# Attention row maxima transposed whole and split into two parts out of PSUM, and an inner maximum joined over two columns

## The reference

```python
x = x + _L0_xattn_ref(_layernorm(x), ctx, ...)   # cross attention without values
x = x + _L0_ffn_ref(_layernorm(x), w_gate, w_up, w_down)
x = x + _L1_xattn_ref(_layernorm(x), ctx, ctx)
x = x + _L1_ffn_ref(_layernorm(x), gate_w, w0, w1, wo, ...)   # 8 experts, 2 per token

# inside _L0_ffn_ref, before each of its matmuls:
def act_quant(x):
    scale = 127.0 / jnp.clip(jnp.max(jnp.abs(x), axis=-1, keepdims=True), EPS)
    return jnp.clip(jnp.round(x * scale), -128.0, 127.0) / scale

# _L1_xattn_ref: 32 query heads of 16 dims, 8 key/value heads, 4 query heads on each
scores = jnp.einsum('bkgsd,bktd->bkgst', qh, kh) / scale
weights = jax.nn.softmax(scores, axis=-1)
out = jnp.einsum('bkgst,bktd->bkgsd', weights, vh)
```

## Time and profile before

| | us |
|---|---|
| median of three runs | 1726.64 |
| lowest and highest | 1716.98, 1729.44 |
| the profiled execution | 1717.66 |
| its span, first to last instruction | 1715.8 |
| busy PE, DVE, ACT, POOL | 1581.2, 957.0, 715.6, 700.8 |
| attention (first to last maximum and its end) | about 495 to 952 |
| mixture of experts, to the end | about 952 to 1716 |

### The profile page before, as it was taken

One profiled execution on the slowest core, in us unless ns is written; L12 is line 12 of the kernel. 1 busy time (PEld: TensorE's weight loads), 2 busy tenths in 40 slices (PEclk: granted clock), 3 DMA queues, 4 the chain that ended last, 5 costly groups with the idle time before them and its releaser, 6 DMA issues. The chain is left out here.

```text
span 1715.8 us, 24430 instructions
## 1 busy us (share of the span) xinstructions
PE 1581.2 (92%) x8105; PEld 1051.9 (61%) x8106; DVE 957.0 (56%) x1571; ACT 715.6 (42%) x1157; POOL 700.8 (41%) x478
## 2 busy tenths in 40 slices
PE   6869999999779999999988399999999999999998
PEld 4555656575533433433333378788878888878886
DVE  6998889797878897888874512222222222222221
ACT  6884646464537777777765111111111111111111
POOL 1124342543503125362464482680754080740065
PEclk9879999999988999999998799999999999999999
DMA  9189600000321445253520343241441041431078
GB/s 356 76 305 386 236 1 1 1 0 1 108 65 46 121 126 148 81 150 89 146 97 33 143 136 114 83 172 37 172 156 53 25 178 31 172 126 34 25 131 213
DMA packets 90945, 196.17 MB, mean 114 GB/s; under 512 B 7153, under 2 KB 9074, under 8 KB 90226
## 3 DMA queue, kind: packets, MB, share of 16 engines
q1 hardware_dynamic: 71746, 156.68, 27.3%
q0 software_dynamic: 7168, 17.04, 4.4%
q10 hardware_dynamic: 11952, 21.43, 3.8%
HBM read 113.28 MB, written 81.32 MB: 113 GB/s over the span
## 5 line engine op out<-in xcount | busy, mean ns | idle before, releaser
L2002 DVE TENSOR_REDUCE neg_max<-psum 128x2 f32<-128x1024 f32 x256 | 300.7, 1219 | 54.6 <-PE psum L2642 53.6
L1388 ACT ACTIVATE probabilities<-psum 128x512 f32<-128x512 f32 x512 | 270.8, 601 | 105.4 <-PE psum L2669 101.1
L2120 DVE TENSOR_TENSOR expert_inner<-psum,expert_inner 128x512 f32<-128x512 f32 x78 | 53.9, 691 | 393.9 <-ACT expert_inner L1481 393.9
L2812 PE MATMUL psum<-expert_weight_parts,sorted_tokens_t_first 128*128 x624 | 252.4, 405 | 9.9 <-POOL expert_weight_parts L1020 6.5
L2813 PE MATMUL psum<-expert_weight_parts,sorted_tokens_t_first 128*128 x624 | 248.5, 398 | 0.0
L2814 PE MATMUL psum<-expert_weight_parts,sorted_tokens_t_second 128*128 x624 | 248.5, 398 | 0.0
L1481 ACT ACTIVATE expert_inner<-psum 128x512 f32<-128x512 f32 x78 | 46.7, 599 | 401.8 <-PE psum L2814 401.8
L2669 PE MATMUL psum<-query_rows,key_rows 50*128 50x512 f32 x512 | 180.7, 449 | 8.1 <-ACT probabilities L1388 5.6
L2642 PE MATMUL psum<-key_rows,query_rows 48*128 48x512 f32 x512 | 174.3, 499 | 13.8 <-DVE neg_max L2002 11.2
L2812 PEld LDWEIGHTS psum<-expert_weight_parts,sorted_tokens_t_first 128*128 128x128 f32 x624 | 119.0, 191 | 38.8 <-issue 11.9
L2680 PE MATMUL psum<-probabilities,value_and_one 128*32 128x512 f32 x1024 | 142.2, 629 | 0.0
(11 more groups left out here) (304 smaller groups left out, 2952.3 us busy)
## 6 DMA issues: line engine op xcount, KB each, us to landing
sorted_x<-zero_rows SPq DMA_DIRECT2D x9, 3960.0 KB, 30.4
w_of_odd_expert<-in_L_ffn_w SPq DMA_DIRECT2D x8, 2048.0 KB, 9.1
wo_of_expert<-in_L_ffn_wo SPq DMA_DIRECT2D x7, 2048.0 KB, 8.7
query_rows<-query_rows_of_units SPq DMA_DIRECT2D x64, 192.0 KB, 3.6
w_of_even_expert<-in_L_ffn_w SPq DMA_DIRECT2D x6, 2048.0 KB, 12.1
sorted_tokens<-sorted_x ACTq DMA_DIRECT2D x39, 264.0 KB, 2.8
sorted_y<-expert_out ACTq DMA_DIRECT2D x39, 256.0 KB, 2.1
query_rows_of_units<-dims_first SPq DMA_DIRECT2D x32, 256.0 KB
```

The source lines that it names most:

```text
L1388: nc.scalar.activation(prob[t % 2][:, i * SEQ:(i + 1) * SEQ], bank[4 + n % 3], ACT.Exp, scale=HD ** -0.5).then_inc(c_e, 1)
L2002: nc.vector.tensor_reduce(of_pair[:, p, st, :], ring(("max", (m, i))).rearrange("p (h n) -> p h n", h=2), AX.X, ALU.max, negate=True).then ...
L2120: nc.vector.tensor_tensor(h, bank[2 * half + 1], h, ALU.mult).then_inc(e_h, 1)
L2812: nc.tensor.matmul(out_bank, hi[:, cols], w_r[:, bass.ds(w_at, 512)], start=start, stop=False)
```

## The change

The maxima are transposed as they are, 16 columns of `nm`, as soon as the eight reductions are done (PE waits for `c_red` in place of `c_np`). `neg_max_split` and `nm_parts` with its memset go. The split is made by DVE out of PSUM: a copy to `first` (signals `c_nhi`), a wait for it, and a subtraction of `first` from the PSUM tile to `second` (signals `c_nsb`). SP issues one DMA for the first part's rows of both halves behind `c_nhi`, and one for the second part's behind `c_nsb`. In `inner_scales` the two columns are joined by one `tensor_reduce` over the two columns.

```diff
             def neg_max_rows(m):
-                sp.wait_ge(c_nsb, m + 1)
-                for h in range(2):
-                    row = 64 * h + 3 * HD
-                    sp.dma_start(q_r[m % 4][row:row + 2, :].bitcast(F32).rearrange("p (t n) -> p t n", n=P),
-                                 nm_t[m % 2][16 * h:16 * h + 16, :].bitcast(F32)).then_inc(c_nmd[m % 4], 16)
+                for part, (made, of) in enumerate(((c_nhi, nm_t[m % 2][0]), (c_nsb, nm_t[m % 2][1]))):
+                    sp.wait_ge(made, m + 1)
+                    rows = q_r[m % 4][3 * HD + part::64, :].bitcast(F32)
+                    sp.dma_start(rows.rearrange("h (t n) -> h t n", n=P),
+                                 of[:].bitcast(F32)).then_inc(c_nmd[m % 4], 16)
...
-                c.step(nc.vector.tensor_tensor(am2[:, s], am2_half[:, 0:1], am2_half[:, 1:2], ALU.max))
+                c.step(nc.vector.tensor_reduce(am2[:, s], am2_half[:], AX.X, ALU.max))
...
-                if there(m):
-                    neg_max_split(m)
...
-                dve.wait_ge(c_red, 8 * (m + 1))
-                dve.wait_ge(c_nt, m)
-                c.step(nc.vector.tensor_copy(parts[:, :, 0, :], of_head))
-                nc.vector.tensor_tensor(parts[:, :, 1, :], of_head, parts[:, :, 0, :], ALU.subtract).then_inc(c_np, 1)
...
             def neg_max_out(m):
+                of = ring(("negmax", m))[0:2 * ST * 2, 0:P]
+                first, second = nm_t[m % 2]
                 dve.wait_ge(c_nt, m + 1)
                 if m >= 2:
                     dve.wait_ge(*neg_max_loaded(m - 2))
-                nc.vector.tensor_copy(nm_t[m % 2][:], ring(("negmax", m))[0:32, 0:P]).then_inc(c_nsb, 1)
+                nc.vector.tensor_copy(first[:], of).then_inc(c_nhi, 1)
+                dve.wait_ge(c_nhi, m + 1)
+                nc.vector.tensor_tensor(second[:], of, first[:], ALU.subtract).then_inc(c_nsb, 1)
...
             def neg_max_transposed(m):
                 job = ("negmax", m)
-                pe.wait_ge(c_np, m + 1)
+                pe.wait_ge(c_red, 8 * (m + 1))
                 take(job, c_nsb, m + 1)
-                nc.tensor.transpose(ring(job)[:, 0:P], nm_parts[:].bitcast(F32), ident[:]).then_inc(c_nt, 1)
+                nc.tensor.transpose(ring(job)[0:2 * ST * 2, 0:P], nm[m % 2][:], ident[:]).then_inc(c_nt, 1)
```

More of the change, by code:

```diff
@@ L243, in network @@
         nm = [small.tile(f"neg_max{i}", [P, ST * GROUP]) for i in range(2)]
-        nm_parts = small.tile("neg_max_parts", [P, P], F32R)
-        nm_t = [small.tile(f"neg_max_rows{i}", [32, P], F32R) for i in range(2)]
+        nm_t = [[small.tile(f"neg_max_{part}_rows{i}", [2 * ST * 2, P], F32R) for part in ("first", "second")] for i in range(2)]
         att_r = small.tile("attended_rsum", [P, ST * GROUP])
@@ L364, in network @@
         c_rows, c_nmd = [sem(f"c_rows{i}") for i in range(4)], [sem(f"c_nmd{i}") for i in range(4)]
-        c_mx, c_red, c_np, c_nt, c_nsb = sem("c_mx"), sem("c_red"), sem("c_np"), sem("c_nt"), sem("c_nsb")
+        c_mx, c_red, c_nhi, c_nt, c_nsb = sem("c_mx"), sem("c_red"), sem("c_nhi"), sem("c_nt"), sem("c_nsb")
         c_s, c_e, c_pv, c_oe, c_at, c_eo, c_v = (sem("c_s"), sem("c_e"), sem("c_pv"), sem("c_oe"), sem("c_at"),
@@ L708, in routing_constants @@
             def routing_constants():
-                sp.wait_ge(c_ones, 6)
+                sp.wait_ge(c_ones, 5)
                 sp.dma_start(gw[:].rearrange("p (k e) -> p k e", k=DC)[:, :, 0:EXPERTS],
@@ L2216, in phase_c @@
                 dve.wait_ge(c_xt, CTX_CHUNK + 1)
-                nc.vector.memset(nm_parts[:].bitcast(F32), 0.0).then_inc(c_ones, 1)
                 nc.vector.memset(gw[:], 0.0).then_inc(c_ones, 1)
@@ L2222, in phase_c @@
                 queries_deviation(BATCH - 1)
-                dve.wait_ge(c_ones, 6)
+                dve.wait_ge(c_ones, 5)
                 for u in range(UNITS + 1):
```

3 lines of the change are left out of this document (removed).

## The result

| | us |
|---|---|
| before, median of six runs beside the changed kernel | 1724.05 (1716.98 to 1729.44) |
| after, median of six runs | 1707.05 (1697.96 to 1708.86) |
| ratio | 0.9889, 95% interval 0.9862 to 0.9916 |
| the profiled execution after | 1707.91, span 1706.1 |

The changed kernel is 1.1% faster, 17.0 us at the medians, where the prediction had 8.0. The measured time, 1707.05, lies inside the stated range of 1706 to 1728, near its fast end; the gain is twice the one forecast, and three terms of the sum had the wrong size, which the part on the prediction takes up one by one.

A forecast was written before the change was run, and what follows sets the result against it. PE was taken as the bound in steady attention (busy 98.10 of 100 us), with time won there reaching the end whole. Terms -1 - 1 - 5.0 - 0.8 - 0.2 = -8.0 us from 1726.64 gave 1718.6, range 1706 to 1728.

The forecast's parts named there:

- the inner maximum: L1891 in phase_b, stalled beside POOL: its replacement by a reduction wins -0.2 us, bound -2.25.
- the regular units: Steady attention, 29 units: split leaves the place ahead of the reductions; -1 us in all, bounds -7.5 and +7.5.
- the stalls of the split: L2031's subtraction held up beside POOL: -5.0 us for the one at 879.15 and -0.8 for the rest.
- the small stalls: L2031's remaining stalls, 1.7 us together on DVE, half counted as reaching PE: -0.8 us.
- A slip of up to 0.26 us against the weight load: Tile 3 in a regular unit: c_nsb comes 0.33 us later, so tile 3 can start at R + 0.74.
- The rival of this name: Late c_nsb decides: tile 3 waits 0.26 us a unit, giving 1727.1, or 1730.6 with a dearer subtraction; chance 0.12.
- The long stall: L2031's 4.50 us subtraction at 879.15 behind POOL's L1020 goes, and its unit with it shortens: -5.0 us.
- The rival that the stall lands elsewhere: L1020 meets L2074 longer, 3 to 4 us, so the 5.0 shrinks to 1 to 2: 1722 to 1723; chance 0.18.
- by that row the stall moves on to L1892: phase_b: the one-column TENSOR_SCALAR behind the inner maximum stalls like four-column L1991, leaving some 0.1 us a tile.
- The start: First two units, where DVE sets the pace: 3 splits of 0.30 us and a memset less; -1 us, bounds 0 and -1.2.
- The anchor: Forecast counted from 1726.64, the median of the runs shown, 9 us above the profiled execution.
- clock case: Fewer waits spare slow-clock stretches, 3 to 10 us more, plus the inner-maximum and regular-unit bounds: 1700 to 1712; chance 0.22.

The follow-up runs named there:

- After with small scatters: The changed kernel with the eight indirect DMAs of each of batches 0 and 1 replaced by plain 16 x 16 DMAs; 0.9877 of before.
- before with small scatters: The kernel before with the eight indirect DMAs of each of batches 0 and 1 replaced by plain 16 x 16 DMAs; 0.9997 of before.
- two reductions there: The changed kernel with two small reductions of the 16 columns where the old split stood; 0.9960 of before.
- wide transpose: The changed kernel with neg_max in tiles of 128 columns, 112 of them zero, all transposed (also called 128 columns); 0.9882 of before.
- one more copy: The changed kernel with one more copy of 16 x 128 out of PSUM ahead of the second part; 0.9857 of before.
- three copies: The changed kernel with three more copies of 16 x 128 out of PSUM ahead of the second part; 1.0018 of before.
- split put back: The changed kernel with the old split's copy and SBUF subtraction back in their place, written where nobody reads; 0.9979 of before.
- the table's first four rows: Profiles of before, before run again (0.9982), before with plain small DMAs for scatters (0.9997), and before with only the inner maximum changed (0.9969).
- after again: The changed kernel, unchanged, run and profiled a second time; 0.9887 of before.
- attention only: The kernel before with the new handling of the maxima but the old inner maximum; 0.9921 of before.
- scatters later: The changed kernel with POOL's two scatters of batch 0 in units 17 and 18 in place of 15 and 16; 0.9871 of before.

## Why the prediction was right or wrong

**The sum, by its terms.** The prediction had which changes win, and three sizes wrong: the inner maximum (-0.2, measured -5.3), the regular units (-1, measured -7.0) and, the other way, the stalls of the split (-5.8, some -3.7). Undoing and separating gives 5.3 us for the inner maximum and 13.5 for the attention, at the medians. What the 13.5 are made of has to come from single profiles. After with small scatters against before with small scatters is the pair that no scatter disturbs: 4.8 us up to the first reciprocal, 10.4 in units 1 to 26, 4.6 in 27 to 29, nothing behind, 19.8 in all. 3.4 of the 10.4 is one unit of that execution of before (unit 21, 16.82 for 13.40) at a mean clock of 0.70, which leaves 7.0. And 1.8 of these are unit 9 alone, 15.26 for 13.49, whose mean clock was 0.89 in every profile of the old attention and 1.00 in most of the new; a small stall of L2031, 0.46 us at 639.89 in before, stands in that unit, but with two reductions there, which don't stall, it took 15.71, so that its part in the clock isn't shown. Of what the prediction asked to see, L2031's successor near 0.30 us and never long came, the unit around 880 took 15.95 us (some 17 predicted), and "wrong if regular units change by more than 0.2 us" came true.

- *Regular units, -1, and the small stalls, -0.8.* Mis-sized, and the largest miss: 7.0 us over units 1 to 26 in that pair. The bound stood in the prediction (7.5) and I took next to nothing of it. Two steps failed. The 0.26 us that I called "the most a regular unit can win" is the idle time of PE's matmul; the weight load ahead of it had idled 0.58 at the same instant and idles 0.21 now, and a chunk unit won 0.41. And I let PE's busy 98.10 in 100 stand for a bound, where the wide transpose shows that 0.1 us more work of PE a unit costs nothing. Plain units did win little, 0.08. Putting 0.34 us of reductions back took all but 0.02 us of both away, so the place is the cause.
- *"A slip of up to 0.26 us against the weight load"* (the late `c_nsb`). Didn't happen. Tile 3's weights wait 0.20 us and its matmul none; one more copy costs 0 and 0.05 us a unit. The prediction took 0.14 us from DVE's end to PE's next start, but it counted from L2037's start at 593.76, and the row of the reduction ends at 593.85, 0.05 ahead of PE. The signal came at R + 0.58 and the weights at R + 0.63, not R + 0.74. The rival of this name needed 0.24 us a unit beyond that and is refuted at this size; three copies show that it exists 0.3 us further on.
- *The long stall, -5.0.* Right for the execution in which it was read: unit 27 took 21.41 us in before and 15.95 in after. But it was no constant of the kernel. One of four profiles of the old attention shows it, and 0.2 us of relative timing decides; the others have the 1.2 to 1.4 us of the copy, which cost unit 27 nothing. In the timed runs the split's stalls, with the small ones, are worth some 3.7 us (split put back against two reductions), where the prediction had 5.0 and 0.8. Over the profiles, units 27 to 29 take 51.1 us on the mean of the table's first four rows and the split put back, and 46.6 on that of after, after again, attention only, one copy more, 128 columns, small scatters and two reductions. That isn't the stall alone, which stands in two of the five. In before with small scatters the excess is in units 28 and 29, 15.88 and 19.35 us at mean clocks of 0.83 and 0.70, where after with small scatters took 13.56 and 17.07 at 1.00 and 0.90. Whether the change has a part in that isn't shown; 128 columns, with the new attention, took 19.26 for unit 29.
- *The rival that the stall lands elsewhere.* It didn't come. The comparison that loses 4.05 us in after lost 4.05 in before, too, so nothing moved to it. The prediction took its 1.14 us at 899.85 for all of it and didn't read on from the earlier trace rows to the next row, 912.80. Only a moved POOL split brought a new stall, 3.43 us in unit 28.
- *The inner maximum, -0.2.* Wrong by the step "by that row the stall moves on to L1892". The stall cost 5.4 us, measured alone, in phase_b; even the bound of 2.25 was too small, since it had three batches at 0.75 us, where each of four batches won 0.9 to 1.7 us. 2.7 of the 5.4 us are in the waits of L2461; where the rest was saved wasn't traced. The nearest row had the right operation and the wrong shape. And that no row shows a one-column TENSOR_SCALAR beside a POOL TENSOR_TENSOR was not so: the trace of before has one at 175.02, four in 0.34 us, shown above. I had named the exception for a single column in one sentence and gave it no weight.
- *The start, -1.* 52.9 us on the mean of the four profiles, 51.0 of the nine: -1.9, outside the stated bounds of 0 and -1.2 by less than the spread of 2 to 3 us, so neither right nor wrong.
- *The anchor.* The median shown first, 1726.64, was 2.6 us above the median of six. This made the forecast slower by as much; the other 9 us of the miss are the terms.

**The Trainium skill on the inner maximum.** In this case's rows a one-column TENSOR_SCALAR takes 0.21 us beside POOL's TENSOR_TENSOR, a four-column one 1.76 to 1.92, and a copy of 16 columns 4.49. The Trainium skill (VectorE: DVE Perf Modes, section Mode 2×_2P — use both read ports for one tensor) says that this two-port mode halves the access pattern along its outermost non-unit dimension; a single column has none. That a single column therefore doesn't take the mode is my reading, which the section doesn't state; the runs agree with it. The prediction had looked at the other page alone.

**The clock.** The prediction's clock case stood at 1700 to 1712 and took in the bounds of regular units and of the inner maximum; the measured 1707.05 lies there. It came for the bounds' reasons more than for the clock's: the two bounds were 7.5 and 2.25, and 7.0 and 5.4 came. But the clock had a part, 1.8 us in unit 9 and up to 4.6 in units 28 and 29 of the pair above, and how much of it is the change's isn't shown.

**What stays open.** Why DVE and ACT get PE's signals about 2 us late near the end of a scatter. Of the ten profiles with the new attention and all its scatters seven show such waits, and in each they end 1.0 to 1.2 us behind the last of four indirect DMAs, which speaks for the scatters. Three of the ten show none (attention only, three copies more, scatters later), so that their absence in the one profile with small scatters proves nothing, and what the DMAs would hold up isn't known. None of the five profiles with work in the old place and all scatters shows one.

## What to carry to other kernels

Read a unit's length against the chain through its ring of buffers, not against an engine's busy share: 0.3 us of DVE ahead of the reduction that PE waits for cost 0.4 us in a unit with transposes and 0.1 in a plain one, 0.3 us behind it nothing to 0.05. When an instruction stalls beside another engine, compare its start with the other's: if they are 0.1 us apart, the stall is a matter of luck in each execution, and its removal is worth its mean. Before carrying a stall over from a nearby row, match its shape as well as its operation, and look for that shape in the whole trace. And before calling a stall new or moved, look for it in the kernel before.

## What the runs showed of the hardware

- Beside POOL's TENSOR_TENSOR on SBUF a DVE copy of 16 columns between SBUF tiles took 4.49 us, a subtraction of 16 columns with two SBUF inputs 4.50, a comparison of 32 columns 4.05, and a TENSOR_SCALAR of four columns up to 1.92 (though 0.17 beside a POOL TENSOR_TENSOR of only four columns, at 31.79 in before). Not held up were a TENSOR_SCALAR of one column (0.21 us, and four with constants in 0.34), a TENSOR_REDUCE (0.155 us), and a TENSOR_TENSOR with one input in PSUM (0.28 us in every unit, and 0.42 in the earlier trace rows).
- Beside POOL's CAST of 2048 columns a DVE copy of 16 columns took 1.21 to 1.36 us, till the cast's end.
- Transposing 16 columns in place of 128 took 0.087 and 0.276 us for weights and matmul, in place of 0.138 and 0.328.
- Near the end of a group of four indirect DMAs of POOL, signals of PE reached DVE or ACT some 2 us late (waits of 1.6 to 2.5 us) in seven of ten profiles of the changed attention.
- One kernel's median lay between 1714.8 and 1726.6 us on four chips, more than most of these edits are worth.
